# RWKV attention beside a mixture of experts, fp32 on one core: z's transpose into PSUM, GpSimd's differences among its scatters, the last batch routed a round ahead, new orders at the prologue and the seams

## The chip, the cores and the metric

The kernel runs on one core of one Trainium2 chip. The metric is the device time in microseconds (us) of one execution, the median of several. Engines are named as the profile does: PE is TensorE's products and PEld its weight loads, DVE is VectorE, ACT is ScalarE, POOL is GpSimd, SP is SyncE, which here only issues DMAs. The granted clock is the one of TensorE, in parts of 2.4 GHz; its two levels are 1.2 and 2.4 GHz.

## What is computed

The input is x, 8 batches of 512 tokens of 512 channels, fp32. It is normalised to xn, and then out = x + attention(xn) + ffn(xn). Cut to what matters:

```python
# attention: a shifted difference mixed in four proportions, four projections, a scan over time
prev = concatenate([xn[:, 1:2], xn[:, :-1]], axis=1)
xx = prev - xn
k, v, r, g = ((xn + xx * tm_i) @ W_i.T for i in "kvrg")
wkv = scan over t of (a + e^u e^k v) / (b + e^u e^k)          # a, b decay by exp(-exp(time_decay))
o = (sigmoid(r) * wkv * sigmoid(g)) @ Wo.T
attention = layernorm(o) * ln_g + ln_b
# ffn: 32 experts, 4 for each token, at most 256 tokens an expert, and one shared expert
z = w_norm * rmsnorm(xn)
probs = softmax(z @ w_router);  w4, sel = top_k(probs, 4)
position of a token in its expert = how many earlier tokens chose that expert   (dropped from 256 on)
y = (silu(z @ w_gate[e]) * (z @ w_up[e])) @ w_down[e]
ffn = sum of w4 * y over the 4  +  sigmoid(z @ w_shared_gate) * (silu(z @ sw_gate) * (z @ sw_up)) @ sw_down
```

## The kernel before

Each product of fp32 matrices is made of three products of rounded parts. A number is split in a high part, rounded to the type fp32r by ScalarE (`mix_hi`, `z_hi`, `weight_hi`), and a low part, the difference of the number and its high part, which GpSimd or VectorE subtracts (`mix_lo`, `z_lo`, `weight_lo`). TensorE adds low x high, high x low and high x high.

The program has three stages that share SBUF and the eight PSUM banks. The order of the work is written out by hand for each engine, and semaphores tie the engines together; an engine takes its instructions strictly in order.

**Project stage** (0 to 492 us), one round for each batch b. The channels lie in four chunks of 128 (k) and the tokens in four tiles of 128 (j). For the next batch the statistics of x are taken (`norm_stats`), GpSimd makes scales of them (`norm_scales`), ScalarE makes xn (`make_xn`), TensorE transposes it into banks 4 and 5 (`turn_xn`), ScalarE copies it to `xnT` (`keep_turned`), VectorE makes the shifted difference xx (`shift_difference`) and, for K, V, R and G in turn, the mixed operand `mixf` (`make_mix`), which is split into `mix`. `project` runs 24 products for each half of each of K, V, R and G, so 192 a round; a half needs the four chunks of `mix` one after the other, and of K also the gates of the batch before (`make_gate`, which free the banks 0 to 3). z in transposed form is made in four chunks by VectorE (`make_zf`: xnT x norm x the turned row scale), into the two buffers `zf` in SBUF, split into `zT` (hi by ScalarE, lo by VectorE: `make_zT` gives their order), stored for the output stage, and multiplied with the router's weights (`score`) into `sb`, which lies in bank 4. `turn_score`, `choose`, `count` and `assign` turn the scores into slots, and GpSimd issues 16 indirect DMAs a batch, each of which writes 128 token numbers into the table of slots (`scatter`). Of them 7 stand between G's and K's differences (SOME), 4 behind K's, and the last 5 in the next round (MORE = 11).

The rounds are: a first one, three turns of a loop over two rounds each, and a last one. In the last round the work of the last batch is as in the others, but its routing starts with the score behind K's first half, and the first expert's transposes (`first_turn`) stand before the last quarter of G's second half; they need the table, which is read when all scatters have landed, and the rows gathered by it.

**Expert stage** (492 to 928 us), one expert after the other. **Output stage** (928 us to the end), eight rounds of the shared expert in 11 slices f, with the scan, the experts' rows (`gather`, `add_expert`) and the attention's projection between them. In its first round the weights of slice f + 2 are loaded and split (`gate_lo` on VectorE, `weight_lo` on GpSimd, `weight_hi` on ScalarE); in the later ones they are there.

In the profile's rows `mix<-mixf,mix` on POOL is `mix_lo` (L356), `slot_tokens<-token,slot` a scatter, `sr<-sr,bank` on DVE a gate, `zT_lo` the low part of z, `s_wg` on DVE `gate_lo`.

## Time and profile before

| | us |
|---|---|
| time before, median of 3 runs (lowest to highest) | 1764.3 (1762.25 to 1766.29) |
| the profiled execution | 1764.3 |
| its span, first to last instruction | 1762.5 |
| TensorE busy | 1665.3 |
| VectorE busy | 1291.8 |
| GpSimd busy | 899.2 |
| ScalarE busy | 660.3 |
| mean granted clock of TensorE | 0.98 of full |

The profile is one execution. Its rows give start and duration in us from the first instruction on, and in square brackets how long the engine sat idle before and what released it. A group of like instructions stands in one row with its count. The project stage takes 28% of the span, the expert stage 25%, the output stage 47%.

### The profile page before, as it was taken

What the parts mean: (1) busy time and instruction counts of PE and PEld (TensorE: products, weight loads), DVE (VectorE), ACT (ScalarE), POOL (GpSimd) and SP (SyncE); (2) the same over time, 40 slices, a digit from 0 to 9 for tenths busy, and PEclk for the clock granted to TensorE, in tenths of its full rate; (3) what the DMA queues carried; (4) which work ended last, traced back from release to release, by engine and by line L of the source; (5) the groups of instructions that cost most, each with busy time, mean ns of one, the idle gap of its engine ahead of it and who ended that gap; (6) DMA issues with size and microseconds to landing.
All of it is one profiled execution on the core that took longest, in us unless ns stands there. A gap on an engine that the chain in (4) does not pass through costs nothing.

```text
span 1762.5 us, 26296 instructions
## 1 busy us (share of the span) xinstructions
PE 1665.3 (94%) x8496; PEld 1412.4 (80%) x8496; DVE 1291.8 (73%) x1828; ACT 660.3 (37%) x1090; POOL 899.2 (51%) x735
## 2 busy tenths in 40 slices
PE   5888989988899999999998799999999999999998
PEld 4666778777689999999996688888788888888887
DVE  7898898989645555555557978687686768778776
ACT  4444445454356665666653322112121212112121
POOL 6587777778644444444536645244353525344251
PEclk9999999999999999999999999999999999999999
DMA  4353324423466666666677655554554434343431
GB/s 156 144 192 120 120 96 167 167 96 119 148 240 234 219 241 245 242 219 236 245 244 229 209 202 186 173 174 145 187 167 156 129 132 129 123 151 108 155 105 45
DMA packets 123082, 299.38 MB, mean 170 GB/s; under 512 B 20524, under 2 KB 31788, under 8 KB 118384
## 3 DMA queue, kind: packets, MB, share of 16 engines
q1 hardware_dynamic: 103392, 264.34, 42.2%
q0 software_dynamic: 19456, 33.67, 6.7%
q8 instruction: 44, 0.72, 0.2%
q14 instruction: 46, 0.38, 0.1%
q10 hardware_dynamic: 144, 0.26, 0.1%
HBM read 233.61 MB, written 81.36 MB: 179 GB/s over the span
## 4 chain that ended last, share of the span: by engine, by line
PE 71%; DVE 16%; issue 6%; DMA 2%; ACT 2%; POOL 1%; DVEq 0%; SPq 0%; POOLq 0%; ACTq 0%
PE bank L1896 24%; PE bank L1274 15%; PE bank L1910 12%; PE bank L1301 8%; PE bank L1927 5%; PE bank L928 4%; DVE zT_lo L640 3%; DVE mixf L664 2%; PE bank L1266 2%; DMA z_rows<-z 1%; POOL slot_tokens L368 1%; DVE seen L716 1%; DVE xx L656 1%; PE bank L888 1%; DVE zf L633 1%
## 5 line engine op out<-in xcount | busy, mean ns | idle before, releaser
L928 PE MATMUL bank<-mix,w 128*128 128x512 f32 x1536 | 378.0, 405 | 39.4 <-DVE sr L685 32.4
L928 PEld LDWEIGHTS bank<-mix,w 128*128 128x128 f32 x1536 | 298.1, 196 | 110.1 <-DVE sr L685 30.9
L1896 PE MATMUL bank<-s_zT,s_wg 128*128 128x512 f32 x1056 | 256.6, 392 | 12.5 <-DVE s_wg L1800 11.8
L1896 PE MATMUL bank<-s_zT,s_wu 128*128 128x512 f32 x1056 | 255.8, 391 | 3.3 <-DVE s_act_g L1705 1.9
L1910 PE MATMUL bank<-s_wd,s_h 128*128 128x512 f32 x1056 | 254.1, 389 | 0.7 <-DVE s_h L1711 0.6
L1896 PEld LDWEIGHTS bank<-s_zT,s_wg 128*128 128x128 f32 x1056 | 198.7, 189 | 57.2 <-DVE s_wg L1800 14.4
L1896 PEld LDWEIGHTS bank<-s_zT,s_wu 128*128 128x128 f32 x1056 | 198.7, 188 | 46.5 <-POOL s_wu L1568 2.9
L1910 PEld LDWEIGHTS bank<-s_wd,s_h 128*128 128x128 f32 x1056 | 198.3, 188 | 42.7 <-issue 1.0
L1095 POOL TENSOR_TENSOR e_wg<-e_g_in,e_wg 128x1408 fp32r<-128x1408 f32 x31 | 100.3, 3236 | 210.5 <-ACT e_wg L1119 210.5
L356 POOL TENSOR_TENSOR mix<-mixf,mix 128x512 fp32r<-128x512 f32 x124 | 172.1, 1422 | 54.7 <-ACT mix L446 54.6
L1531 POOL DMA_INDIRECT s_picked<-y_rows,s_slot x128 | 142.5, 1114 | 84.3 <-DVE s_total L1761 44.6
L1629 ACT ACTIVATE s_h<-s_act_g 128x512 fp32r<-128x512 f32 x88 | 55.6, 632 | 292.0 <-DVE s_act_g L1705 292.0
L368 POOL DMA_INDIRECT slot_tokens<-token,slot x128 | 138.2, 1079 | 52.0 <-issue 37.6
L1618 ACT ACTIVATE s_act_g<-bank 128x512 f32<-128x512 f32 x88 | 52.6, 597 | 292.0 <-PE bank L1896 292.0
L1274 PE MATMUL bank<-e_xT,e_wg 128*128 128x256 f32 (+1 forms) x1152 | 152.2, 282 | 0.0
L1274 PE MATMUL bank<-e_xT,e_wu 128*128 128x256 f32 (+1 forms) x1152 | 152.1, 282 | 0.0
L1274 PEld LDWEIGHTS bank<-e_xT,e_wg 128*128 128x128 f32 (+1 forms) x1152 | 144.3, 180 | 3.0 <-DVE e_xT L1213 0.4
L1274 PEld LDWEIGHTS bank<-e_xT,e_wu 128*128 128x128 f32 (+1 forms) x1152 | 142.1, 180 | 0.0
L1301 PE MATMUL bank<-e_wd,e_h 128*128 128x512 f32 (+1 forms) x576 | 140.1, 396 | 0.0
L1761 DVE SCALAR_TENSOR_TENSOR s_total<-s_picked,s_rec,s_total 128x512 f32<-128x512 f32 x128 | 132.4, 1034 | 3.4
L1551 POOL TENSOR_TENSOR s_att<-s_gate,s_att 128x512 fp32r<-128x512 f32 x32 | 46.2, 1443 | 165.3 <-ACT s_att L1644 165.3
L446 ACT ACTIVATE mix<-mixf 128x512 fp32r<-128x512 f32 x128 | 77.2, 629 | 133.3 <-DVE mixf L664 127.7
(157 smaller groups left out, 2464.3 us busy)
## 6 DMA issues: line engine op xcount, KB each, us to landing
s_wu<-wu_split SPq DMA_DIRECT2D x77, 512.0 KB, 3.4
e_g_in<-in_w_gate SPq DMA_DIRECT2D x32, 704.0 KB, 4.6
e_u_in<-in_w_up SPq DMA_DIRECT2D x32, 704.0 KB, 6.0
e_d_in<-in_w_down SPq DMA_DIRECT2D x32, 512.0 KB, 6.8
y_rows<-e_y SPq DMA_DIRECT2D x32, 512.0 KB, 2.9
s_zT<-zT_parts SPq DMA_DIRECT2D x16, 1024.0 KB, 7.1
x_in<-in_x SPq DMA_DIRECT2D x32, 256.0 KB, 4.8
zT_parts<-zT_hi SPq DMA_DIRECT2D x8, 1024.0 KB, 6.1
```

Of the source, the lines that this page charges most:

```text
L356: pool.tensor_tensor(mix[:, i % 2, k, 1, :], mixf[:, k, :], mix[:, i % 2, k, 0, :].bitcast(F32), ALU.subtract).then_inc(lo_made, 1)
L368: pool.indirect_dma_start(d["slots"], bass.IndirectOffsetOnAxis(ap=slot[:, at:at + 1], axis=0), token[:, at // TOPK:at // TOPK + 1], None, ...
L446: act.activation(mix[:, i % 2, k, 0, :], mixf[:, k, :], ACT.Copy).then_inc(hi_made, 1)
L928: last = pe.matmul(pj[m][:], w[i][:, w_part, k, m * P:(m + 1) * P], mix[:, i % 2, k, x_part, :], start=(k == 0 and q == 0), stop=(k == KC ...
L1095: pool.tensor_tensor(wg[half][:, 1, :], g_in[half][:], wg[half][:, 0, :].bitcast(F32), ALU.subtract).then_inc(wg_lo, 1)
L1274: last = pe.matmul(gu[f][0:m, which, :], w[half][:, w_part, k * F + f0:k * F + f0 + m], xT[half][:, x_part, k, :], start=(q == 0 and k == ...
L1301: last = pe.matmul(yp[c][:], h[0:m, f, h_part, c * P:(c + 1) * P], wd[half][0:m, w_part, f, :], start=(f == 0 and q == 0), stop=(f == NF - ...
L1531: pool.indirect_dma_start(picked[:, k, :], None, d["y_flat"], bass.IndirectOffsetOnAxis(ap=slot[:, j * TOPK + k:j * TOPK + k + 1], axis=0) ...
L1761: dve.scalar_tensor_tensor(total[:, j, :], picked[:, k, :], rec[:, at:at + 1], total[:, j, :], ALU.mult, ALU.add).then_inc(picked_used, 1)
L1896: last = pe.matmul(into[:], w[:, w_part, k, :], zT[:, x_part, k, :], start=(q == 0 and k == 0), stop=(q == 2 and k == KC - 1))
L1910: last = pe.matmul(yp[j][:], h[:, i, h_part, j * P:(j + 1) * P], wd[f][:, w_part, :], start=(f == 0 and q == 0), stop=(f == NFS - 1 and q ...
L1927: last = pe.matmul(ob[j % 2][:], att[m][:, x_part, j * P:(j + 1) * P], wo[m][:, w_part, :], start=(m == 0 and q == 0), stop=(m == KC - 1 a ...
```

## The change

1. `zf` is no longer in SBUF: it is the pair of PSUM banks 4 and 5, in which the transposes of xn and the score also lie. The transposes of the next batch wait for the subtractions that read it (`zl_made`), and the first of z waits until the score is copied out (`score_kept`).
2. GpSimd's differences of R and K alternate with scatters, one each (`mix_lo_among`); 4 instead of 7 scatters stand before K's differences.
3. Round 1 and round 6 are written out beside the loop (two turns instead of three). In round 1 the four `make_z` of batch 1 stand behind the statistics of batch 2, not before the round; 11 scatters of batch 0 are split by K's differences. In round 6 (`tail`) z of batch 7 is made ahead of K's mixes, its score stands between the halves of G and its turn inside G's second half; in the last round `choose` comes first.
4. In the last round GpSimd makes V's differences only, behind the leftover scatters; R's move to VectorE.
5. The prologue: two of four x tiles are loaded by ScalarE's queue, the constants by SP's, K's first differences by VectorE, the weights of R and G are split in four parts, and V's and z's work changes places.
6. In the first output round the weights' splitting is moved ahead of other work on all three engines, and VectorE's first scan waits for three setup steps instead of four.

```diff
-    zf = at("zf", [P, 2, T], 184)
+    zf = xt
...
         first_round()
-        with eng.Fori(0, B // 2 - 1) as h:
-            one_round(h * 2 + 1, 1)
+        one_round(1, 1, second=True)
+        with eng.Fori(0, B // 2 - 2) as h:
             one_round(h * 2 + 2, 0)
+            one_round(h * 2 + 3, 1)
+        one_round(B - 2, 0, tail=True)
         last_round()
```

SP's queue:

```diff
-        for j in range(NT):
-            load_x(0, j)
-        for i in (K_, V_):
-            load_weight(i)
+        load_x(0, 0)
+        load_x(0, 1)
+        load_weight(K_)
+        sp.dma_start(const[:], d["const"]).then_inc(c_loaded, 16)
+        load_weight(V_)
```

GpSimd:

```diff
+        def mix_lo_among(b, i, of, at):
+
+            for k in range(KC):
+                mix_lo(b, i, (k,))
+                scatter(of, at + k, at + k + 1)
...
-            mix_lo(b, R_)
-            scatter(b - 1, MORE, NT * TOPK)
+            mix_lo_among(b, R_, b - 1, MORE)
+            scatter(b - 1, MORE + KC, NT * TOPK)
             mix_lo(b, G_)
             scatter(b, 0, SOME)
-            mix_lo(b + 1, K_)
-            scatter(b, SOME, MORE)
+            mix_lo_among(b + 1, K_, b, SOME)
+            scatter(b, SOME + KC, MORE)
 
         def last_round():
+            scatter(LAST - 1, MORE, NT * TOPK)
             mix_lo(LAST, V_)
-            scatter(LAST - 1, MORE, NT * TOPK)
-            mix_lo(LAST, R_)
             scatter(LAST, 0, NT * TOPK)
 
-        SOME, MORE = 7, 11
+        SOME, MORE = 4, 11
```

ScalarE, prologue and first round:

```diff
         for k in range(KC):
             mix_hi(0, K_, k)
+            weight_hi(R_, (k,))
...
-            for k in range(KC):
-                mix_hi(0, V_, k)
-            weight_hi(R_)
             exp_k(0, 0)
             exp_k(0, 1)
-            weight_hi(G_)
+            for k in range(KC):
+                mix_hi(0, V_, k)
```

VectorE, z and the prologue:

```diff
+                wait(dve, score_kept, b)
             wait(dve, zl_made, n - 1)
-            dve.scalar_tensor_tensor(zf[:, k % 2, :], xnT[half][:, k, 1:T + 1], norm_col[:, k:k + 1], rb[:],
+            dve.scalar_tensor_tensor(zf[k % 2][:], xnT[half][:, k, 1:T + 1], norm_col[:, k:k + 1], rb[:],
...
         for k in range(KC):
             shift_difference(0, 0, k)
+            if k:
+                mix_lo(0, K_, k - 1)
             make_mix(0, 0, K_, k)
+        mix_lo(0, K_, KC - 1)
+        weight_lo(V_)
```

VectorE, round 1 and round 6:

```diff
             norm_stats(b + 1)
+            if second:
+                for j in range(NT):
+                    make_z(1, 1, j)
...
+            if tail:
+                make_zT(LAST, FIRST_HALF)
             for k in range(KC):
                 make_mix(b + 1, 1 - half, K_, k)
-            make_zT(b + 1, 1 - half)
+            if not tail:
+                make_zT(b + 1, 1 - half)
```

TensorE:

```diff
+            wait(pe, zl_made, b * KC)
...
-            project(b, G_, 1)
+            if tail:
+                score(LAST)
+            project(b, G_, 1, {3: lambda: turn_score(LAST)} if tail else {})
```

The first output round, on GpSimd, ScalarE and VectorE:

```diff
+                if zero(b) and f + 2 < NFS:
+                    weight_lo(U, f + 2)
...
                 hidden_hi(b, half, f)
+                if zero(b) and f + 2 < NFS:
+                    weight_hi(G, f + 2)
+                    weight_hi(U, f + 2)
...
                 hidden_lo(b, half, f)
-                fill(f)
                 if zero(b) and f + 2 < NFS:
                     gate_lo(f + 2)
+                fill(f)
...
-            dve.wait_ge(setup, 4)
+            dve.wait_ge(setup, 3)
```

What stands in a row, at three places. GpSimd between the slots of a batch and the next round, first in the loop of before, where `mix<-mixf,mix` is a difference and `slot_tokens` a scatter:

```order
L368 DMA slot_tokens<-token,slot 8192x1 x7
L355 ISA
L356 TENSOR_TENSOR mix<-mixf,mix 128x512
L355 REGISTER_ALU
L356 TENSOR_TENSOR mix<-mixf,mix 128x512
L355 REGISTER_ALU
L356 TENSOR_TENSOR mix<-mixf,mix 128x512
L355 REGISTER_ALU
L356 TENSOR_TENSOR mix<-mixf,mix 128x512
L368 DMA slot_tokens<-token,slot 8192x1 x4
```

and on GpSimd in the changed kernel, at the same place of round 6:

```order
L372 DMA slot_tokens<-token,slot 8192x1 x4
L358 TENSOR_TENSOR mix<-mixf,mix 128x512
L372 DMA slot_tokens<-token,slot 8192x1
L358 TENSOR_TENSOR mix<-mixf,mix 128x512
L372 DMA slot_tokens<-token,slot 8192x1
L358 TENSOR_TENSOR mix<-mixf,mix 128x512
L372 DMA slot_tokens<-token,slot 8192x1
L358 TENSOR_TENSOR mix<-mixf,mix 128x512
L372 DMA slot_tokens<-token,slot 8192x1 x9
```

Seven scatters ahead of four differences have become four ahead of four pairs; the nine at the end are the pair's last one, three of the same batch and the five that the last round begins with.

VectorE at the end of round 6, before (the loop's end; `zf` and `zT_lo` are z, `sr` the gates):

```order
L664 SCALAR_TENSOR_TENSOR mixf<-xx,keep_const,xnT_66 128x512 x2
L50 REGISTER_ALU
L633 SCALAR_TENSOR_TENSOR zf<-xnT_66,keep_const,bank 128x512 x2
L640 TENSOR_TENSOR zT_lo<-zf,zT_hi 128x512
L633 SCALAR_TENSOR_TENSOR zf<-xnT_66,keep_const,bank 128x512
L640 TENSOR_TENSOR zT_lo<-zf,zT_hi 128x512
L633 SCALAR_TENSOR_TENSOR zf<-xnT_66,keep_const,bank 128x512
L640 TENSOR_TENSOR zT_lo<-zf,zT_hi 128x512 x2
L685 TENSOR_TENSOR sr<-sr,bank 128x512 x4
```

and on VectorE in the changed kernel, from the shifted differences of batch 7 to the first copy of its logits:

```order
L673 TENSOR_TENSOR xx<-xnT_66 128x512 x4
L650 SCALAR_TENSOR_TENSOR bank<-xnT_66,keep_const,bank 128x512 x2
L657 TENSOR_TENSOR zT_lo<-bank,zT_hi 128x512
L650 SCALAR_TENSOR_TENSOR bank<-xnT_66,keep_const,bank 128x512
L657 TENSOR_TENSOR zT_lo<-bank,zT_hi 128x512
L650 SCALAR_TENSOR_TENSOR bank<-xnT_66,keep_const,bank 128x512
L657 TENSOR_TENSOR zT_lo<-bank,zT_hi 128x512 x2
L681 SCALAR_TENSOR_TENSOR mixf<-xx,keep_const,xnT_66 128x512 x4
L702 TENSOR_TENSOR sr<-sr,bank 128x512 x2
L709 COPY lg<-bank 128x136
```

z reads and writes a bank now and has moved ahead of K's mixes, and `choose` (from `lg` on) has moved between the first and the second pair of gates.

TensorE in the last round of before (`w_56` to `w_59` are the weights of K, V, R and G, `zT_lo` and `zT_hi` the score, `oh` its turn, `chosen` and `seen` the count):

```order
L928 MATMUL bank<-mix,w_56 128x512 x24
L888 MATMUL bank<-zT_lo,wr 68x512 x4
L888 MATMUL bank<-zT_hi,wr 68x512 x4
L928 MATMUL bank<-mix,w_56 128x512 x12
L897 MATMUL bank<-keep_const,oh 128x68 x4
L928 MATMUL bank<-mix,w_56 128x512 x12
L928 MATMUL bank<-mix,w_57 128x512 x18
L905 MATMUL bank<-chosen,before 128x128
L906 MATMUL bank<-seen,ones 128x128
L928 MATMUL bank<-mix,w_57 128x512 x30
```

and on TensorE in the changed kernel, from the middle of G of batch 6 to V of batch 7:

```order
L957 MATMUL bank<-mix,w_59 128x512 x24
L917 MATMUL bank<-zT_lo,wr 68x512 x4
L917 MATMUL bank<-zT_hi,wr 68x512 x4
L957 MATMUL bank<-mix,w_59 128x512 x18
L926 MATMUL bank<-keep_const,oh 128x68 x4
L957 MATMUL bank<-mix,w_59 128x512 x6
L957 MATMUL bank<-mix,w_56 128x512 x30
L934 MATMUL bank<-chosen,before 128x128
L935 MATMUL bank<-seen,ones 128x128
L957 MATMUL bank<-mix,w_56 128x512 x18
L957 MATMUL bank<-mix,w_57 128x512 x48
```

The score of batch 7 has moved from K of batch 7 into G of batch 6, and the count from V into K.

## Rows read from the trace of the kernel before

**Rows 1.** The page, busy time, share of the span and instructions of each engine.

```profile
PE 1665.3 (94%) x8496; PEld 1412.4 (80%) x8496; DVE 1291.8 (73%) x1828; ACT 660.3 (37%) x1090; POOL 899.2 (51%) x735
```

**Rows 2.** Windows by stage: length, busy by engine, PEclk, DMA share, GB/s.

```profile
0.00:152.30 152.30, 111.79 (x472) 86.28 (x472) 131.23 (x219) 68.37 (x110) 102.83 (x96) 0.94 0.39 142
152.30:429.30 277.00, 253.28 (x1131) 205.78 (x1131) 247.14 (x461) 131.11 (x227) 215.55 (x201) 0.95 0.34 129
429.30:492.60 63.30, 52.36 (x215) 41.91 (x215) 38.85 (x77) 22.34 (x34) 39.99 (x35) 0.88 0.47 169
492.60:927.50 434.90, 434.90 (x3129) 410.86 (x3129) 239.53 (x383) 268.31 (x446) 196.79 (x96) 1.00 0.68 239
927.50:1050.00 122.50, 107.37 (x446) 84.64 (x445) 100.04 (x93) 38.12 (x66) 67.07 (x57) 0.97 0.64 211
```

**Rows 3.** Timeline of PE, a steady round: start, us, what [idle before <-releaser].

```profile
207.38 7.36 PE L928 MATMUL bank<-mix,w 128*128 128x512 f32 x24 [4.06 <-DVE sr L685]
...
235.61 22.04 PE L928 MATMUL bank<-mix,w 128*128 128x512 f32 x96
```

**Rows 4.** Timeline of DVE, the same stretch.

```profile
227.01 3.86 DVE L716 TENSOR_TENSOR seen<-seen,chosen 128x32 bf16<-128x32 bf16 x4
...
244.26 0.17 DVE L738 TENSOR_TENSOR slot<-s,s 128x16 uint32<-128x16 f32 x1
...
254.18 5.82 DVE L640 TENSOR_TENSOR zT_lo<-zf,zT_hi 128x512 fp32r<-128x512 f32 x1
```

**Rows 5.** Timeline of POOL, the same stretch.

```profile
204.17 1.26 POOL L368 DMA_INDIRECT slot_tokens<-token,slot  x1 [0.17 <-issue]
...
213.22 5.87 POOL L356 TENSOR_TENSOR mix<-mixf,mix 128x512 fp32r<-128x512 f32 x4 [3.87 <-ACT mix L446]
...
254.43 5.00 POOL L356 TENSOR_TENSOR mix<-mixf,mix 128x512 fp32r<-128x512 f32 x4
```

**Rows 6.** Groups by line: count, busy us, mean ns of one, idle before.

```profile
L368 POOL DMA_INDIRECT slot_tokens<-token,slot x128 | 138.2, 1079 | 52.0 <-issue 37.6 <-DVE slot L738 14.3
...
L1213 DVE TENSOR_TENSOR e_xT<-bank,e_xT 128x512 fp32r<-128x512 f32 x64 | 41.2, 686 | 29.6 <-ACT e_xT L1134 29.6
...
L680 DVE TENSOR_TENSOR ekv<-ek,bank 128x512 f32<-128x512 f32 x32 | 20.4, 678 | 0.0
```

**Rows 7.** Timeline of PE, the end of the last round.

```profile
488.61 1.98 PE L1266 MATMUL bank<-keep_const,e_rows 128*128 128x128 f32 x8 [8.23 <-DMA e_rows<-z_rows,keep_index]
```

**Rows 8.** Timeline of POOL, the end of the last round.

```profile
478.75 0.97 POOL L368 DMA_INDIRECT slot_tokens<-token,slot  x1 [0.30 <-issue]
```

**Rows 9.** Timeline of all engines, the opening.

```profile
14.64 0.43 SPq L271 DMA_DIRECT2D wr_staged<-in_Wr  x1
...
21.32 4.36 PE L928 MATMUL bank<-mix,w 128*128 128x512 f32 x12 [3.95 <-POOL mix L356]
```

**Rows 10.** Timeline of DVE, the first round.

```profile
37.38 3.81 DVE L640 TENSOR_TENSOR zT_lo<-zf,zT_hi 128x512 fp32r<-128x512 f32 x1 [1.17 <-ACT zT_hi L439]
...
58.86 3.44 DVE L613 SCALAR_TENSOR_TENSOR z<-xn,r,norm_w 128x512 f32<-128x512 f32 x2 [2.51 <-DMA z_rows<-z]
```

**Rows 11.** Timeline of PE, the first two rounds.

```profile
48.32 1.98 PE L888 MATMUL bank<-zT_lo,wr 128*68 128x512 f32 x4 [7.61 <-DVE zT_lo L640]
...
98.29 7.42 PE L928 MATMUL bank<-mix,w 128*128 128x512 f32 x24 [2.26 <-DVE sr L685]
```

**Rows 12.** DMA issues of the first 60 us: line, count, KB, us to landing.

```profile
wr_staged<-in_Wr SPq DMA_DIRECT2D x1, 1024.0 KB, 7.1
```

**Rows 13.** Timeline of DVE, the first output round.

```profile
934.78 1.23 DVE L1728 TENSOR_TENSOR_SCAN s_b_sum<-keep_decay,s_ek 128x512 f32<-128x512 f32 x1 [5.16 <-POOL s_picked L1580]
...
998.23 4.69 DVE L1711 TENSOR_TENSOR s_h<-s_act_g,s_h 128x512 fp32r<-128x512 f32 x1 [0.70 <-ACT s_h L1629]
```

**Rows 14.** Timeline of PE, the same stretch.

```profile
937.85 4.46 PE L1896 MATMUL bank<-s_zT,s_wu 128*128 128x512 f32 x12 [1.92 <-DVE s_act_g L1705]
...
1009.89 0.50 PE L1896 MATMUL bank<-s_zT,s_wg 128*128 128x512 f32 x1 [3.90 <-DVE s_wg L1800]
```

More of the change, by code:

```diff
@@ L294, in first_round, with one_round @@
                 load_x(2, j)
-            for j in range(NT):
-                store_z(1, j)
-        def one_round(b, half):
+        def one_round(b, half, second=False, tail=False):
+            if second:
+                store_zT(1)
             store_gate(b - 1)
-            store_zT(b)
+            if not second:
+                store_zT(b)
+            if second:
+                for j in range(NT):
+                    store_z(1, j)
             store_ek(b)
-            if not (isinstance(b, int) and b + 2 >= B):
+            if not tail:
                 for j in range(NT):
@@ L526, in first_round, with one_round @@
                 z_hi(1, k)
-        def one_round(b, half):
+        def one_round(b, half, second=False, tail=False):
             gate_g(b - 1, 2)
@@ L554, in one_round @@
             gate_r(b, 1)
+            if tail:
+                for k in range(KC):
+                    z_hi(LAST, k)
             mix_hi(b + 1, K_, 0)
@@ L560, in one_round @@
             mix_hi(b + 1, K_, 3)
-            for k in range(KC):
-                z_hi(b + 1, k)
+            if tail:
+                keep_score(LAST)
+            else:
+                for k in range(KC):
+                    z_hi(b + 1, k)
             gate_g(b, 0)
@@ L776, in first_round @@
             keep_scales(0, 0)
+            for k in range(KC):
+                make_mix(0, 0, R_, k)
+            make_ekv(0, 0)
+            make_ekv(0, 1)
             dve.wait_ge(n_loaded, 16)
@@ L779, in first_round @@
             make_z(0, 0, 1)
-            make_ekv(0, 0)
-            make_ekv(0, 1)
-            for k in range(KC):
-                make_mix(0, 0, R_, k)
+            make_ekv(0, 2)
+            make_ekv(0, 3)
             make_z(0, 0, 2)
             make_z(0, 0, 3)
-            make_ekv(0, 2)
-            make_ekv(0, 3)
             choose(0)
@@ L801, in first_round, with one_round @@
             keep_scales(1, 1)
-            for j in range(NT):
-                make_z(1, 1, j)
-        def one_round(b, half):
+        def one_round(b, half, second=False, tail=False):
             make_gate(b - 1, 2)
@@ L810, in one_round @@
             norm_stats(b + 1)
+            if second:
+                for j in range(NT):
+                    make_z(1, 1, j)
             for k in range(KC):
@@ L829, in one_round @@
                 shift_difference(b + 1, 1 - half, k)
+            if tail:
+                make_zT(LAST, FIRST_HALF)
             for k in range(KC):
                 make_mix(b + 1, 1 - half, K_, k)
-            make_zT(b + 1, 1 - half)
+            if not tail:
+                make_zT(b + 1, 1 - half)
             make_gate(b, 0)
@@ L836, in last_round @@
         def last_round():
+            choose(LAST)
             make_gate(LAST - 1, 2)
@@ L840, in last_round @@
                 make_mix(LAST, FIRST_HALF, V_, k)
-            for k in range(KC):
-                make_mix(LAST, FIRST_HALF, R_, k)
-            choose(LAST)
             assign(LAST)
-            make_ekv(LAST, 0)
-            make_ekv(LAST, 1)
+            for pair in ((0, 1), (2, 3)):
+                for k in pair:
+                    make_mix(LAST, FIRST_HALF, R_, k)
+                if pair[0] == 0:
+                    make_ekv(LAST, 0)
+                    make_ekv(LAST, 1)
+                for k in pair:
+                    mix_lo(LAST, R_, k)
+            make_ekv(LAST, 2)
+            make_ekv(LAST, 3)
             for k in range(KC):
                 make_mix(LAST, FIRST_HALF, G_, k)
-            make_ekv(LAST, 2)
-            make_ekv(LAST, 3)
             for k in range(KC):
@@ L954, in first_round, with one_round @@
             project(0, G_, 1)
-        def one_round(b, half):
+        def one_round(b, half, second=False, tail=False):
             project(b, K_, 0)
@@ L1675, in one_round @@
                 if zero(b) and f + 2 < NFS:
-                    for which in (G, U, D):
-                        weight_hi(which, f + 2)
+                    weight_hi(D, f + 2)
                 if zero(b) and f == 1:
```

94 lines of the change are left out of this document (45 added, 49 removed).

## Prediction

> **What bounds the kernel now.** I read the page first: TensorE is busy 94% of the span, VectorE 73%, GpSimd 51% [rows 1]. That is an average over stages, so the windows by stage come next [rows 2]. The eight rounds of the first stage have the losses: in the five steady rounds (K of batch 2 to K of batch 7, 277.0 us, 55.4 each) TensorE is idle 23.7 us and its mean granted clock is 0.95; in the opening 40.5 us are idle at 0.94, in the last round 10.9 at 0.88, and in the first output round 15.1 at 0.97. From 492.6 to 927.5 TensorE is never idle, so the expert stage can't give anything, and the output rounds after 1050.0 are not touched.
>
> In a steady round the PE timeline shows where the loss sits: the K product starts 4.06 us late, released by the gate product on VectorE (`sr`, L685), and its 24 products take 7.36 us, while 96 later ones take 22.04, that is 5.51 per 24 [rows 3]. So the engine comes out of the idle time at the lower level of its clock (1.2 instead of 2.4 GHz for some of it) and loses another 1.85 us. From 207.38 to the end of G at 257.65 are 50.27 us; less 1.85 the engine needs **48.4 us** a round.
>
> Why the gate is late stands in the VectorE timeline: one `zT_lo` subtraction, at 254.18, takes 5.82 us [rows 4], while GpSimd runs four differences, of 5.00 us together, beside it [rows 5]. VectorE work with an operand in PSUM is not stretched beside GpSimd: `ekv<-ek,bank` has a mean of 678 ns over 32, `e_xT<-bank,e_xT` 686 over 64 [rows 6].
>
> **The change, part by part.** *z in PSUM.* The same 32 multiplications and 32 subtractions run. The subtraction has the form of `e_xT`, so I price it at 0.69; once a round 5.82 - 0.69 = 5.13 us go. By the Trainium skill, page "SBUF — State Buffer", section "SBUF: two separate sides", GpSimd and a VectorE instruction with two SBUF inputs exclude each other for a whole instruction, so a PSUM operand frees it; that agrees with the rows. But by the same rule it would wait for one GpSimd instruction, a quarter of 5.0 us, not for four; then only 1.25 us a round would be saved. The row with 5.82 us decides, and the sum takes 5.13. The new waits (xn's transposes for `zl_made`, z for `score_kept`) ask for events half a round old; I cost them at nothing. If that cover were gone, the transposes would wait out the subtractions, about 3 us.
>
> *The steady round.* VectorE sets it now: 55.4 - 5.13 = 50.3 us. What is late next? TensorE needs 48.4. GpSimd is busy 215.55 / 5 = 43.1 [rows 2], and 16 scatters add 0.3 each between them: 47.9, without its waits for others. So VectorE's 50.3 stays the longest, by a thin margin. The new GpSimd order doesn't add work: from `slot` on, 4 scatters of about 1.3, then four pairs of difference and scatter at 1.25 + 1.43. The last K difference comes 5.3 + 3 x 2.68 + 1.25 = 14.6 us after `slot` (244.4); before it was 254.43 + 5.00 = 259.4, 15.0 after it. TensorE wants it 4.1 us into K, at T + 52.5 in terms of the K start T; it is ready at T + 37.1 + 14.6 = T + 51.7. That fits with 0.8 us to spare. GpSimd's V differences begin about 1 us later than now (213.22 has 3.87 idle before it). Spread differences stretch the `seen` additions (3.86 for four [rows 4], nearly one difference each) less often: perhaps 1 us better. I take **50.3** (48.8 to 53). For four rounds: 221.5 to 201.2, -20.3.
>
> *Round 6, which scores batch 7.* It gets 8 score products and 4 transposes (2.2 us, an estimate: 8 x 0.23 by the 96 in 22.04, and 0.4) and they stand ahead of the last quarter of G; z of batch 7 is then made ahead of the K mixes, after some 43 us of VectorE work, when TensorE arrives at about the same time. 48.4 + 2.2 + 1.9 for meeting late = 52.5 against 55.5, -3.0.
>
> *Last round.* Now 63.3 us, of which 8.23 idle for the gathered rows [rows 7], 2.7 idle elsewhere, the rest slow clock and work. The chain behind the 8.23 is 16 scatters in a row, the last at 478.75 [rows 8], then table, index, gather: first transpose at 488.61, 9.86 after the last scatter starts. After: `slot` is ready some 16 us into the round, but GpSimd first runs four leftover scatters, five more of batch 6 and then the V differences. It leaves the tail's four at T + 8, the five at T + 14.5, V from 14.5 to 19.5. TensorE wants V at T + 12.8, so it **loses about 3 to 5 us in a place where it loses nothing now**. The 16 scatters of batch 7 start at T + 19.7, the last one at 38.9, the transposes at T + 48.8; TensorE comes there at T + 47.2. Adding 4.0 from the first transpose to the first expert product gives 52.8: -10.5 (-4 to -14). `choose` ahead of the gates also holds K's second half by some 2 us; that is in it.
>
> *Opening.* To K of batch 2: 152.3 us. The first product starts at 21.3 [rows 9]. From there two rounds at 48.4 would end at 118, so 34 us can be had at most. Of those, VectorE's two `zT_lo` beside GpSimd's weight differences (3.81 for the first of them [rows 10]) leave TensorE idle for 7.61, and z's stores and slow clock cost 2.26 idle and 7.42 - 5.51 = 1.9 in K's second half [rows 11]. Following the new order by these durations: K runs from 20 to 34, V's first half to 39.5 (V's low weights, on VectorE, are ready at 29), score to 41.5, V's second half to 47, R with its transposes to 60, G to 72.6. Then K of batch 1 is paced by pairs of difference and scatter and ends its first half at 80, and score(1) starts there instead of at 92.4. In round 1 VectorE sets the pace: z's four products now stand behind the statistics, and K of batch 2 comes at 125 by VectorE, 130 with what such a chain leaves out. -22 (-12 to -28). A cost in it: ScalarE's rounding of R's first quarter stands behind the first K rounding and needs the weights, which are issued at 14.64 and land 7.1 later, at 21.7 [rows 9, 12]. That delays K's second chunk by 1.5 us; counted.
>
> *Seam to the output.* VectorE waits 5.16 us for GpSimd's memset of `picked`, the fourth setup step, where it will ask for three [rows 13], and TensorE then waits 1.92 and takes 4.46 us for 12 products, 2.8 at full clock [rows 14]: -3.5. Of the remaining idle time much is released by `gate_lo` (3.90 at 1009.89), but VectorE's chain is full there, with stretched instructions as the 4.69 at 998.23 [rows 13]. Moving `gate_lo` ahead of the fill work lets TensorE do a gate product earlier and then wait for `hidden`; I give it 2.5. The roundings moved ahead of `silu` can hold ScalarE while pieces arrive, so -6 in all (+3 to -14).
>
> **Sum.** -20.3 - 3.0 - 10.5 - 22 - 6 = -61.8. The profiled execution is 1764.3 us (span 1762.5, 1.8 around it), which is the median of the three runs. 1764.3 - 61.8 = 1702.5, say **1703 us**.
>
> **Rivals.**
> 1. *GpSimd becomes the bound.* For: 47.9 us plus waits for ScalarE's roundings is close to 50, and pairs leave it no room. A period of 53 gives 4 x 53 + 55 = 267 instead of 277 (-10), -5 in the last round, -22 and -6: **1721**. Against: it waits 3.87 us before V now.
> 2. *The stall moves.* K's and V's mixes read two SBUF operands. If one of them waits out the differences that z's subtraction waited for, rounds stay at 55; only the opening, the last round and the seam gain: 1764.3 - 2 - 14 - 8 - 6 = **1734**. Against: the differences are single between scatters, so one waits 1.25 at most.
> 3. *The opening gives little,* held by z's stores (VectorE waits 2.51 for one [rows 10]) or R's weights: -10 instead of -22, **1715**.
> 4. *Slower.* Alternation sets VectorE's and GpSimd's instructions against each other all the time. Four V differences take 5.87 instead of 5.0 where mixes run beside them [rows 5]. If all four groups do (+0.9 each) and 16 scatters grow by 0.4 each, GpSimd's round is 47.9 + 3.6 + 6.4 = 57.9: +2.5 a round over now, five times, and the other terms shrink to -8 together: **1769**. It decides from 0.3 us more a scatter. Against: a scatter's mean is 1.08 us over all 128 now [rows 6].
>
> **How the numbers follow.** Forecast 0.66, rival 1 0.16, rival 2 0.05, rival 3 0.09, rival 4 0.04. The range should leave out 2 in 10: the forecast's own terms go from 1678 to 1739 if all ends come together, 1687 to 1722 without that; with rivals 1 and 3 inside and rival 2 at its edge I give 1687 to 1733. A measurement of this kernel tells about 0.2% (3.5 us) from no change. Faster by more: forecast and rivals 1 to 3, 0.95 less a little for several going wrong, 0.94; slower 0.04; within 0.02.
>
> **What would show it.** `zT_lo` at a mean near 0.7 us instead of 1.9, no long one; K starts 50 us apart with next to no idle before them and the clock near 1.0 in the rounds; K of batch 2 near 130, the first expert product near 436; TensorE waiting for V's differences in the last round; the setup wait gone. Wrong if K starts stay 53 or more apart, if GpSimd is released by no one in the rounds and TensorE waits for its `mix`, or if the first output round still takes 122 us.

## The result, and the profile after

The changed kernel takes **1735.1 us** (median, 1733.8 to 1736.0), the kernel before 1764.1 in the same measurement; the ratio is 0.983, with an interval of 0.982 to 0.985. It is faster by 29 us, not by the 61.8 that the forecast gave, and lies 2 us above the upper end of its range. The profiled execution has a span of 1734.2 us.

Page of after, part 1, against [rows 1]:

```profile
PE 1653.1 (95%) x8496; PEld 1402.8 (81%) x8496; DVE 1275.4 (74%) x1836; ACT 661.5 (38%) x1093; POOL 885.7 (51%) x733
```

Windows of after, cut at the places of [rows 2]: the opening up to K of batch 2 in two windows, four steady rounds, round 6, the last round, the experts, the first output round. Columns as there:

```profile
17.20:80.14 62.94, 51.91 (x226) 40.10 (x226) 55.79 (x104) 32.34 (x54) 38.41 (x33) 0.97 0.38 137
80.14:141.92 61.78, 51.52 (x227) 41.10 (x227) 58.38 (x107) 30.28 (x53) 50.25 (x46) 0.94 0.36 136
141.92:352.37 210.45, 198.67 (x904) 159.24 (x905) 193.71 (x369) 104.86 (x182) 172.17 (x161) 0.99 0.39 140
352.37:407.90 55.53, 52.36 (x238) 41.93 (x239) 50.53 (x99) 26.61 (x47) 42.17 (x40) 0.97 0.39 152
407.90:468.04 60.14, 48.72 (x204) 38.99 (x202) 36.16 (x75) 22.76 (x34) 37.38 (x35) 0.91 0.41 143
468.04:903.00 434.96, 434.96 (x3128) 410.90 (x3129) 239.56 (x383) 268.36 (x446) 196.80 (x96) 1.00 0.67 239
903.00:1020.80 117.80, 105.07 (x446) 83.60 (x446) 101.32 (x93) 37.53 (x66) 67.20 (x57) 0.99 0.68 219
```

So every stage gained less than forecast, the seam by the least: opening 10.4 us (152.3 to 141.9; forecast 22), four steady rounds 10.7 (221.1 to 210.45; forecast 20.3), round 6 and the last round 3.5 together (119.1 to 115.7; forecast 13.5), the first output round 4.7 (122.5 to 117.8; forecast 6 with what lies around it). The experts take 434.96 as before.

The one step on which most rested is right. Group of `zT_lo` over the whole run, by line: count, busy us, mean ns; it was 1894 ns before the change:

```profile
L657 DVE TENSOR_TENSOR zT_lo<-bank,zT_hi 128x512 fp32r<-128x512 f32 x32 | 22.0, 688 | 0.6
```

But a round gained less than these 5.13 us. Timeline of a steady round of after, PE, then DVE, then POOL, to be held against [rows 3 to 5]:

```profile
193.62 7.34 PE L957 MATMUL bank<-mix,w 128*128 128x512 f32 x24 [2.34 <-DVE sr L702]
...
221.82 22.58 PE L957 MATMUL bank<-mix,w 128*128 128x512 f32 x96
246.72 3.50 PE L957 MATMUL bank<-mix,w 128*128 128x512 f32 x14 [2.32 <-DVE sr L702]
```

```profile
201.50 6.23 DVE L681 SCALAR_TENSOR_TENSOR mixf<-xx,keep_const,xnT 128x512 f32<-128x512 f32 x4 [0.62 <-POOL mix L358]
...
213.12 2.70 DVE L733 TENSOR_TENSOR seen<-seen,chosen 128x32 bf16<-128x32 bf16 x4
215.93 2.69 DVE L629 SCALAR_TENSOR_TENSOR z<-xn,r,norm_w 128x512 f32<-128x512 f32 x2
...
220.92 0.79 DVE L629 SCALAR_TENSOR_TENSOR z<-xn,r,norm_w 128x512 f32<-128x512 f32 x1 [1.11 <-DMA z_rows<-z]
...
232.18 0.17 DVE L755 TENSOR_TENSOR slot<-s,s 128x16 uint32<-128x16 f32 x1
...
236.38 4.13 DVE L681 SCALAR_TENSOR_TENSOR mixf<-xx,keep_const,xnT 128x512 f32<-128x512 f32 x4
```

```profile
238.65 1.30 POOL L358 TENSOR_TENSOR mix<-mixf,mix 128x512 fp32r<-128x512 f32 x1
240.12 1.26 POOL L372 DMA_INDIRECT slot_tokens<-token,slot  x1 [0.17 <-issue]
```

From `slot` to the next K start it is 14.5 us, where it was 18.55 (244.26 to 262.81 before): 4.0 less instead of 5.13, since the four K mixes take 4.13 us and not 2.74. From `seen` to `slot` it is 19.1 instead of 17.25. The additions of `seen` got 1.16 shorter, as forecast, but the two z behind them 1.27 longer (1.42 before), and VectorE then waits 1.11 for z's store and stands another 1.60 in front of the fourth z, released by nothing that the profile shows; this 1.60 stands in one of the four rounds. The other rounds are 51.7, 53.7 and 51.95 us long.

The first row of VectorE above is R's four mixes, which read two SBUF operands. GpSimd's block of V's differences (200.15 to 205.19) runs beside them, and they take 6.23 to 6.24 us in three of the four rounds. Before, in the same place:

```profile
218.20 3.43 DVE L664 SCALAR_TENSOR_TENSOR mixf<-xx,keep_const,xnT 128x512 f32<-128x512 f32 x4
```

They end 14.1 us after K's start as they did before (207.73 - 193.62; 221.63 - 207.38 is 14.25): VectorE comes to them earlier and loses it there.

The end of the last round, PE, DVE and POOL:

```profile
422.73 33.16 PE L957 MATMUL bank<-mix,w 128*128 128x512 f32 x138 [3.26 <-POOL mix L358]
464.05 1.98 PE L1297 MATMUL bank<-keep_const,e_rows 128*128 128x128 f32 x8 [8.16 <-DMA e_rows<-z_rows,keep_index]
```

```profile
422.61 3.78 DVE L754 CAST token<-keep_const 128x4 uint32<-128x4 f32 x1 [3.93 <-DMA slot_tokens<-token,slot]
```

```profile
421.38 4.97 POOL L358 TENSOR_TENSOR mix<-mixf,mix 128x512 fp32r<-128x512 f32 x4
427.30 0.99 POOL L372 DMA_INDIRECT slot_tokens<-token,slot  x1 [0.94 <-DVE slot L755]
434.23 0.98 POOL L372 DMA_INDIRECT slot_tokens<-token,slot  x1 [5.94 <-issue]
...
454.22 0.97 POOL L372 DMA_INDIRECT slot_tokens<-token,slot  x1 [0.30 <-issue]
```

The first scatter stands where the forecast put it (19.4 us after K's start at 407.9; 19.7 forecast), the last one does not: 26.9 us behind the first, not 19.2. So the transposes still wait 8.16 us, as in [rows 7].

### The profile page after: what moved, and what is told of

Same layout as the page of the kernel before. It is cut to its first block, busy times and chain, and to the rows that moved or that the text cites. A ratio compares the mean times of both kernels' runs of the same rounds, so it can differ in the third digit from the quotient of the medians.

```text
span 1734.2 us, 26081 instructions
## 1 busy us (share of the span) xinstructions
PE 1653.1 (95%) x8496; PEld 1402.8 (81%) x8496; DVE 1275.4 (74%) x1836; ACT 661.5 (38%) x1093; POOL 885.7 (51%) x733
## 4 chain that ended last, share of the span: by engine, by line
PE 69%; DVE 14%; issue 8%; POOL 4%; DMA 3%; ACT 2%; DVEq 0%; SPq 0%; POOLq 0%; ACTq 0%
PE bank L1930 24%; PE bank L1305 16%; PE bank L1944 12%; PE bank L1332 8%; PE bank L1961 5%; DVE mixf L681 3%; POOL slot_tokens L372 2%; PE bank L1297 2%; PE bank L957 2%; DMA z_rows<-z 1%; POOL mix L358 1%; DVE bank L650 1%; DVE z L629 1%; DVE s_wg L1834 1%; DVE ekv L697 1%
## 5 line engine op out<-in xcount | busy, mean ns | idle before, releaser
L957 PE MATMUL bank<-mix,w 128*128 128x512 f32 x1536 | 369.4, 398 | 27.5 <-DVE sr L702 11.0
L957 PEld LDWEIGHTS bank<-mix,w 128*128 128x128 f32 x1536 | 289.3, 191 | 97.9 <-DVE sr L702 10.6
L1930 PE MATMUL bank<-s_zT,s_wu 128*128 128x512 f32 x1056 | 256.3, 392 | 13.5 <-DVE s_act_g L1739 11.5
L358 POOL TENSOR_TENSOR mix<-mixf,mix 128x512 fp32r<-128x512 f32 x116 | 154.8, 1353 | 51.5 <-ACT mix L455 50.5
```

The lines of the kernel that those rows point to most:

```text
L358: pool.tensor_tensor(mix[:, i % 2, k, 1, :], mixf[:, k, :], mix[:, i % 2, k, 0, :].bitcast(F32), ALU.subtract).then_inc(lo_made, 1)
L957: last = pe.matmul(pj[m][:], w[i][:, w_part, k, m * P:(m + 1) * P], mix[:, i % 2, k, x_part, :], start=(k == 0 and q == 0), stop=(k == KC ...
L1930: last = pe.matmul(into[:], w[:, w_part, k, :], zT[:, x_part, k, :], start=(q == 0 and k == 0), stop=(q == 2 and k == KC - 1))
```

## The experiments

Each kernel was timed beside the kernel before on the same chip; ratios and intervals are to that one.

### z in PSUM alone, and everything but it

The first run takes the kernel before and moves only z:

```diff
-    zf = at("zf", [P, 2, T], 184)
...
+    zf = xt
...
+                wait(dve, score_kept, b)
...
+            wait(pe, zl_made, b * KC)
```

> The kernel before with one edit of the change alone: zf lies in the two PSUM banks, with its two waits; GpSimd keeps its blocks of four differences. Theory 1 (the pairs of difference and scatter took back what z in PSUM gave): zT_lo falls from 5.82 to 0.7 us in each round, K's four mixes stay at 2.74 us, the K starts stand 50.3 apart, and the first round gains its two long subtractions (6.6 us). Sum 1764 - 6.6 - 6 x 5 = about 1728, faster than the changed kernel (1735). Theory 2 (the stretch moves to other VectorE work wherever GpSimd's differences stand): rounds of 53, about 1745, slower than the changed kernel.

Measured: **1735.1 us**, ratio 0.983 (0.982 to 0.985). That is the time of the whole change. Neither number was met: the rounds behave nearly as theory 1 says (51.2 us, not 50.3), but the last round is 66.4 us long, 3.1 more than before. Timeline of PE and of DVE in this run:

```profile
140.17 5.73 PE L930 MATMUL bank<-mix,w 128*128 128x512 f32 x24 [1.32 <-DVE sr L686]
191.45 5.73 PE L930 MATMUL bank<-mix,w 128*128 128x512 f32 x24 [1.34 <-DVE sr L686]
...
235.24 6.06 PE L930 MATMUL bank<-mix,w 128*128 128x512 f32 x24 [0.60 <-ACT sr L461]
242.63 5.76 PE L930 MATMUL bank<-mix,w 128*128 128x512 f32 x24 [1.33 <-DVE sr L686]
```

```profile
233.29 2.74 DVE L665 SCALAR_TENSOR_TENSOR mixf<-xx,keep_const,xnT 128x512 f32<-128x512 f32 x4
```

K's half starts at the full clock now (5.73 for 24, not 7.36). K of batch 2 comes at 140.17, earlier than in the changed kernel (141.92), and K of batch 6 at 344.93 (352.37). The other parts of the change thus cost 7.4 us up to there. The last two rounds (115.7 us there, 117.8 here) and the seam gave it back. In the last round VectorE now meets R's block of differences with an instruction on 4 numbers a partition, in the middle of the choice, and TensorE waits 7.13 us for the count:

```profile
414.99 4.89 DVE L714 TENSOR_SCALAR keep_const<-keep_const 128x4 f32<-128x4 f32 x1
```

The second run leaves everything of the change but z: `zf` is in SBUF again, the two waits are gone.

> The changed kernel with zf back in SBUF and without the two new waits; all its orders stay. Theory 1 (a VectorE instruction waits out the whole run of GpSimd instructions that follow each other without a gap; between pairs there is one): zT_lo waits for one difference, 1.3 us more, in one or two of four, so a round is 1.3 to 2.6 longer and the time 1743 to 1750. Theory 2 (scatters hold VectorE out as well as differences do): zT_lo waits 5 us as before, 55 a round, about 1760.

Measured: **1755.2 us**, 0.996 (0.995 to 0.997). So z in PSUM is worth 20 us inside the change. The time lies between the theories, above the 1750 of theory 1; the mechanism is that of theory 1, since no instruction waits 5 us:

```profile
247.29 1.39 DVE L656 TENSOR_TENSOR zT_lo<-zf,zT_hi 128x512 fp32r<-128x512 f32 x1
...
249.38 2.05 DVE L656 TENSOR_TENSOR zT_lo<-zf,zT_hi 128x512 fp32r<-128x512 f32 x1
...
252.13 2.63 DVE L656 TENSOR_TENSOR zT_lo<-zf,zT_hi 128x512 fp32r<-128x512 f32 x2
```

Here the four take 6.07 us, against 2.82 with z in PSUM and 7.98 in the kernel before (0.69, 5.82 and 1.47 for two); I had counted one or two that wait, and it is three. Pairs spread the wait over several instructions; with z in SBUF that helps a little, with z in PSUM there is nothing left to help.

### Pairs or blocks on GpSimd

K's differences in one block again, behind seven scatters:

```diff
-            scatter(b, 0, SOME)
-            mix_lo_among(b + 1, K_, b, SOME)
-            scatter(b, SOME + KC, MORE)
+            scatter(b, 0, SOME + 3)
+            mix_lo(b + 1, K_)
+            scatter(b, SOME + 3, MORE)
```

> The changed kernel with K's differences in one block behind seven scatters, as before; R's pairs stay. Theory 1 (K's pairs cost VectorE 1.4 us a round, 4.15 instead of 2.74 for four mixes; a block would fall beside z and the gates, which have an operand in PSUM): rounds of 50.3 instead of 51.7, six times, about 1727. Theory 2 (the block stretches other work as much as the pairs do): 1735, no change.

Measured: **1729.5 us**, 0.981 (0.979 to 0.982): theory 1, with 5.6 of its 8 us. (The gain is against 1735.1; the intervals of the two kernels touch, and the rounds show it.) The rounds are 51.5 us (K of batch 2 at 140.65, of batch 6 at 346.48). DVE in one of them: the K mixes are back at 2.73, and a wait for the store of z shows up.

```profile
220.94 1.48 DVE L629 SCALAR_TENSOR_TENSOR z<-xn,r,norm_w 128x512 f32<-128x512 f32 x2 [2.41 <-DMA z_rows<-z]
...
234.72 2.73 DVE L681 SCALAR_TENSOR_TENSOR mixf<-xx,keep_const,xnT 128x512 f32<-128x512 f32 x4
```

R's differences in a block as well (`mix_lo(b, R_)`, then the five scatters):

> The kernel of the run with K's block (1729.5 us) with R's differences in a block too, as before the change. Theory 1 (R's pairs cost nothing net: the stretch falls on the two z of the first pair, 2.69 instead of 1.41, instead of on the additions of seen, 3.87 instead of 2.70): 1729.5, rounds of 51.2. Theory 2 (the pairs also make the z wait longer for their stores, 2.41 against 0.50 in a round): one of the four rounds gets 1 us shorter, 1727 to 1729. Rival (R's block makes TensorE wait): over 1731.

Measured: **1725.4 us**, 0.977 (0.975 to 0.979), 4 less. DVE:

```profile
210.19 3.87 DVE L733 TENSOR_TENSOR seen<-seen,chosen 128x32 bf16<-128x32 bf16 x4
214.16 1.41 DVE L629 SCALAR_TENSOR_TENSOR z<-xn,r,norm_w 128x512 f32<-128x512 f32 x2
...
218.30 1.51 DVE L629 SCALAR_TENSOR_TENSOR z<-xn,r,norm_w 128x512 f32<-128x512 f32 x2 [1.52 <-DMA z_rows<-z]
```

`seen` and the first two z take 5.28 us together, 5.39 in pairs; the wait for the store is 0.9 shorter. K of batch 6 comes at 343.62 instead of 346.48; of these 2.9 us, 1.8 lie ahead of K of batch 2 (about 138.9 instead of 140.65), and the rounds are 51.2 us. Theory 2, with a larger effect than said; the two intervals just touch.

### The opening

The first round's K differences in a block too, on the kernel with K's block:

```diff
-            mix_lo_among(1, K_, 0, SOME)
-            scatter(0, SOME + KC, MORE)
+            mix_lo(1, K_)
+            scatter(0, SOME, MORE)
```

> The kernel of the run with K's block (1729.5 us) with the first round's K differences in a block as well, behind four scatters. In the changed kernel TensorE takes K's first half of round 1 at the pace of pairs, 2.74 us a chunk instead of 1.66. Theory 1 (the pairs set the opening too): score of batch 1 2.5 us earlier, near 86.8, K of batch 2 near 138, 1727. Theory 2 (VectorE is the bound of the opening: busy 114 of the 125 us from 17.2 on, so what TensorE gains is lost again at the count of batch 1): K of batch 2 at 140.6 or later, 1729.5.

Measured: **1728.4 us**, 0.980 (0.978 to 0.982), against 1729.5. PE:

```profile
86.61 1.14 PE L917 MATMUL bank<-zT_lo,wr 128*68 128x512 f32 x4 [1.18 <-DVE zT_lo L657]
...
114.45 0.29 PE L934 MATMUL bank<-chosen,before 128*128 128x128 bf16 x1 [6.00 <-DVE seen L733]
```

The score of batch 1 comes 2.7 us earlier than in the changed kernel (89.32), its count only 0.5 (114.95, where TensorE waits 5.96). Part of that isn't the edit's: the count of batch 0, which stands ahead of it, is 1.6 us earlier already (62.85, there 64.42). Counted from it, the score comes 1.1 us earlier and the count of batch 1 1.1 us later (51.6, there 50.5), and the score of batch 2 stands at 146.12, in the kernel with K's block at 146.26. VectorE's chain to the choice of batch 1 swallows what TensorE gains: theory 2. The 1.1 us of time are within the noise.

What in that chain is long was asked next, on the joined kernel below. Of z of batch 1 by rows only 8 of 512 channels are made, so this kernel leaves the others out:

> The joined kernel in which the four multiplications that make z of batch 1 by rows take 8 of the 512 channels (so the expert inputs of batch 1 are not computed); all waits stay. Asks what bounds the opening. Theory 1 (VectorE's chain in round 1, z, R's mixes, then the choice, which TensorE waits 6 us for at the count of batch 1): these four took 4.94 + 1.43 us; the count and K of batch 2 come 3 to 5 us earlier. Theory 2 (TensorE or GpSimd): K of batch 2 stays where it is.

Measured: **1723.4 us**, 0.977 (0.976 to 0.978); the joined kernel has 1721.6. The count comes 1.1 us earlier and no more, the score of batch 2 1.2 (143.66, there 144.90): less than theory 1 said, more than theory 2. DVE and POOL in this run:

```profile
94.54 4.56 DVE L629 SCALAR_TENSOR_TENSOR z<-xn,r,norm_w 128x8 f32<-128x8 f32 x2
101.15 0.23 DVE L629 SCALAR_TENSOR_TENSOR z<-xn,r,norm_w 128x8 f32<-128x8 f32 x1 [2.05 <-DMA z_rows<-z]
```

```profile
93.90 5.03 POOL L358 TENSOR_TENSOR mix<-mixf,mix 128x512 fp32r<-128x512 f32 x4
```

Two multiplications of 8 channels take 4.56 us, two of 512 took 5.61 there (a single one of 8 takes 0.23): the first waits until GpSimd's run of four is over, at 98.9. Cutting the work of a waiting instruction gives little, and the wait for the store grows from 1.51 to 2.05 us.

The other wait in that chain is the store. z by rows gets four buffers instead of two, the new ones where `zf` lay:

```diff
-    z = at("z", [P, 2, C], 176)
+    z = at("z", [P, NT, C], 176)
...
-            wait(dve, z_stored[j % 2], (b * 2 + j // 2) * 16)
+            wait(dve, z_stored[j], b * 16)
```

> The joined kernel with four SBUF buffers for z by rows instead of two (the second two in the place that zf left), so that VectorE never waits for a store of z. Theory 1 (VectorE sets the rounds and the opening, so each wait for a store counts): the waits are 0.5 to 2.4 us in a round and 3.8 in the opening; 3 to 8 us less than the joined kernel. Theory 2 (TensorE sets the rounds at 51.2 now: ACT's gate of R and the slow gate product leave it about 2 us idle): under 2 us.

Measured: **1718.6 us**, 0.974 (0.973 to 0.976), 3 less than the joined kernel; the two intervals overlap a little, so the rows have to show it. PE:

```profile
111.14 0.23 PE L934 MATMUL bank<-chosen,before 128*128 128x128 bf16 x1 [0.21 <-DVE seen L733]
...
137.40 5.73 PE L957 MATMUL bank<-mix,w 128*128 128x512 f32 x24 [1.33 <-DVE sr L702]
...
188.18 5.74 PE L957 MATMUL bank<-mix,w 128*128 128x512 f32 x24 [1.33 <-DVE sr L702]
...
201.05 0.41 PE L926 MATMUL bank<-keep_const,oh 68*128 68x68 f32 x4
```

DVE, R's mixes in the round that starts at 188.18:

```profile
196.68 6.24 DVE L681 SCALAR_TENSOR_TENSOR mixf<-xx,keep_const,xnT 128x512 f32<-128x512 f32 x4 [1.24 <-POOL mix L358]
```

The count comes 2.4 us earlier than in the joined kernel (3.4, counted from the count of batch 0) and waits for nearly nothing. Theory 1 at its lower end: rounds of 50.8 us, there 51.2.

### The last round

V's differences of the last round on VectorE, on the changed kernel:

```diff
             scatter(LAST - 1, MORE, NT * TOPK)
-            mix_lo(LAST, V_)
             scatter(LAST, 0, NT * TOPK)
...
+            for k in range(KC):
+                mix_lo(LAST, V_, k)          # VectorE, behind V's mixes
             assign(LAST)
```

> The changed kernel with V's differences of the last round on VectorE instead of GpSimd. Theory 1 (GpSimd's four V differences cost twice: TensorE waits 3.26 us for them, and the copy of token numbers, 3.78 us beside them, holds the slots and with them all 16 scatters): slot near 423 instead of 426.3, the scatters start 3 to 4 us earlier, TensorE's 3.26 gone, first transposes of the expert stage near 460 instead of 464, about 1731. The idle 5.94 us behind the first scatter stays if it comes from the loads of the expert's weights that run then; if it belongs to the V differences it goes too, then 1726. Theory 2 (the last round is bound elsewhere): 1735.

Measured: **1735.8 us**, 0.983 (0.981 to 0.985): no gain. DVE:

```profile
426.54 0.17 DVE L753 CAST token<-keep_const 128x4 uint32<-128x4 f32 x1 [6.71 <-DMA slot_tokens<-token,slot]
```

The copy of the token numbers takes 0.17 us now instead of 3.78, so GpSimd's V differences had stretched it. But it starts no sooner: it waits until the scatters of batch 6 have landed, 7.1 us after the last of them starts (419.48); in the changed kernel it was 2.2 (420.41 to 422.61). Beside them run the store of e^k and the 3 MB of the first expert's weights, issued from 418.3 on; that these make the landing late is a guess at this point. So SP's order was changed, on the kernel with K's block:

```diff
+            first_weights()
             store_gate(LAST - 1)
             store_ek(LAST)
-            first_weights()
```

> The kernel of the run with K's block (1729.5 us) with one more edit: in the last round SP issues the first expert's weights (3 MB) ahead of the stores of the gates and of e^k, some 15 us earlier. Theory 1 (the 6.44 us in which GpSimd stands between the first and the second scatter of batch 7, and the late landing of scatters, come from these loads, which fill the 16 DMA engines from 417 to 434): with the loads over before the scatters begin, the gap falls to 0.3 to 2.9 us, the first transposes of the expert stage come 3.5 to 6 us earlier, 1723.5 to 1726. Theory 2 (the gap belongs to something else, it stands in every kernel so far with at least 2.94): gap 6.4, 1729.5.

Measured: **1726.8 us**, 0.977 (0.976 to 0.979), 2.7 less. POOL, first of the kernel with K's block alone, then with the loads early:

```profile
420.78 0.99 POOL L372 DMA_INDIRECT slot_tokens<-token,slot  x1 [0.94 <-DVE slot L755]
428.21 0.98 POOL L372 DMA_INDIRECT slot_tokens<-token,slot  x1 [6.44 <-issue]
```

```profile
422.06 0.99 POOL L372 DMA_INDIRECT slot_tokens<-token,slot  x1 [0.94 <-DVE slot L755]
426.00 1.32 POOL L372 DMA_INDIRECT slot_tokens<-token,slot  x1 [2.95 <-issue]
...
447.23 0.97 POOL L372 DMA_INDIRECT slot_tokens<-token,slot  x1 [0.30 <-issue]
```

The idle time behind the first scatter falls by 3.5 us and TensorE's wait for the gathered rows from 10.71 to 8.13. The rest, 2.95, stands there however early the loads are; what it is I didn't find. With the loads early V's differences were moved once more, on the joined kernel:

> The joined kernel with V's differences of the last round on VectorE. Alone on the changed kernel this gave nothing: the copy of the token numbers then waited 6.71 us for the scatters of batch 6 to land, beside 4 MB of other transfers. Theory 1 (that wait came from the weights' loads): with the loads early the slot is ready near 16 us into the last round instead of 17.4 and the transposes come 1.5 us earlier, -1.5. Theory 2 (VectorE's own four differences, 3 us, put slot as late): 0 to +1.

Measured: **1722.7 us**, 0.977 (0.976 to 0.979), against 1721.6. From K of batch 6 to the transposes it is 106.5 us instead of 107.2, half of the expected gain, and the time doesn't show it: theory 2. The stretch behind the transposes is 4.5 us longer in this profile, which the edit doesn't touch. Over the profiles of the eleven kernels with the new seam this stretch goes from 1268.3 (joined) to 1276.5 us (V's on VectorE, on the changed kernel), with the same code; why stays open, and a difference of that size between two profiles says nothing of an edit.

### The seam alone

The output round's edits of the change on the kernel before, nothing else:

> The kernel before with one part of the change alone: the new orders of the first output round on GpSimd, ScalarE and VectorE, and three setup steps instead of four. In the changed kernel the stretch from the first expert product to the gate product of the second output round was 4.7 us shorter. Theory 1 (that is this edit): 1764.3 - 4.7 = 1759.6. Theory 2 (the stretch is shorter for other reasons): 1764.

Measured: **1760.0 us**, 0.997 (0.995 to 0.998): 5.2 less, theory 1. TensorE's largest wait in the first output round (total, times, longest), before, then in this run:

```profile
PE bank L1896 <- DVE s_wg L1800: 11.8, 5, 3.9
```

```profile
PE bank L1899 <- DVE s_act_g L1708: 10.9, 6, 2.4
```

The wait changed its name and nearly kept its size; of the one for `s_wg` 0.2 us are left. Most was gained early in the round: TensorE's tenth group of 12 products starts 26.8 us after the first (925.72 to 952.49), where it was 30.9 (927.58 to 958.45), 4.1 of the 4.9 us that the round got shorter. There VectorE's first scan of the stage, released 5.16 us late by `picked` in [rows 13], follows its neighbour without idle time. The run holds the shorter setup wait and the new orders together, so how much is owed to which isn't shown.

### The edits joined

K's and R's blocks, the first round's block and the early loads, in one kernel:

> The changed kernel with four edits together: K's and R's differences in blocks, the first round's K differences in a block behind four scatters, and the first expert's weights issued early. Sum of what the single runs gave: 1735.1 - 5.6 (K's block) - 4.0 (R's block) - 1.1 (first round) - 2.7 (weights) = 1721.7. Rival (K's and R's blocks had already taken what the other two can give): 1725.

Measured: **1721.6 us**, 0.976 (0.975 to 0.978). The single gains add up. That they do so to 0.1 us is luck: each of them is known to 2 to 4 us, and one, the first round's 1.1, may be nothing. With the four buffers of z, 1718.6 us is the fastest kernel of the study, 1% faster than the changed one.

## Why the forecast was too large

- **z in PSUM, steady rounds** (5.13 us a round): right. In the run with z alone the stretch from the first scatter to the next K start falls from 17.55 (245.26 to 262.81) to 12.37 us (230.26 to 242.63), by 5.18. An instruction that waits, waits for GpSimd's run of four to its end. The Trainium skill, page "SBUF — State Buffer", section "SBUF: two separate sides", has an exclusive lock held for one whole instruction; the rows agree with it as to which instructions are freed, not as to how long the others wait.
- **The round's 50.3 us**: too low by 0.9 even with blocks (51.2). TensorE waits 0.6 us for ScalarE's gate and 1.3 for the gate product in each round, and VectorE for z's stores; with four buffers it is 50.8. What is left was overlooked by the forecast and by the runs: R's mixes beside V's block, 6.23 to 6.25 us in three of four rounds with blocks and four buffers too. There they end 14.7 us into the round (202.92 after 188.18), and TensorE has the scores turned at 13.3 (201.46), so the choice starts 1.4 us late. That is an estimate of what another place for V's block could give a round; no run moved it.
- **"The new GpSimd order doesn't add work … perhaps 1 us better"**: this step failed. `seen` gained its 1.16, but I priced no other VectorE instruction that now meets a single difference. The K mixes (+1.4) and the z (+1.3) did. The worry was in rival 2, and I had dismissed it with "one waits 1.25 at most": that is the price in each round, and I left it out of the sum. Rounds of 51.7 to 53.7 are between the forecast and rival 2's 55. GpSimd was not the bound; TensorE waited for its `mix` in no steady round. Blocks in both places give 9.7 us back, 5.7 of them in the four rounds and 3.0 in the opening.
- **Opening** (22): mis-sized. Two long `zT_lo` in the first round and one in the second make 11.7, and z alone measured 12.2. The 10 us for the new order were TensorE's arrivals added up, while the windows show VectorE busy 114.2 of 124.7 us there, time in which its instructions wait for GpSimd included; it was the bound. A gain of TensorE's was lost there (the first round's block), a wait taken from VectorE was not (the four buffers). Rival 3 gave -10 for it, the size that came out, but named VectorE's wait for z's stores and R's weights. Of these the stores were part of it.
- **Last round** (-10.5): the term was mis-sized. V's wait (3.26 us) and the first scatter came as forecast. From the first of the 16 scatters to the last I took 15 x 1.28 = 19.2 us, though the timeline of before had them at 23.5 (455.24 to the row of [rows 8]), 2.94 of it the idle time behind the first; they took 26.9. The first expert's loads fell on them: with the loads early the 16 take 25.2 us, 27.7 without (K's block in both). So 7.7 us were missing in the chain behind which TensorE waits, and the early start of the routing went into it.
- **Round 6** (-3.0): nothing came, 55.5 us. TensorE waits 3.17 us for z of batch 7 ahead of its score.
- **Seam** (-6): about right, 4.7 to 5.2.
- **Slower by alternation** (rival 4) saw that alternation costs, but put the cost on GpSimd: a scatter's mean rose from 1.08 to 1.10 us, not by 0.4, and GpSimd was not the bound. The cost fell on VectorE.
- **The time itself** lies 1 us from rival 2's 1734, by luck. Rival 2 had 2 us for the rounds, 14 for the opening, 8 for round 6 and the last and 6 for the seam; measured are 10.7, 10.4, 3.5 and 4.7. Its mechanism is there in part: K's mixes wait, for one difference a round and not for four.

## What to carry to other kernels

When an instruction waits out another engine's run, free that instruction and then ask where the run should stand so that only freed instructions lie beside it. Here a solid block beside z's PSUM work was better than pairs that meet everything, and the block that stayed beside R's mixes was overlooked. Before crediting a new order with TensorE's idle time, look whether another engine is full in the same window. And take a serial chain from its first to its last row, not from a mean times a count; the idle time inside it is part of it.

## What was not expected of the hardware

- A VectorE instruction can wait much longer than it works: two multiplications of 8 channels took 4.56 us beside a run of four differences, and a copy of 4 numbers a partition with a single SBUF input 3.78 us (until 426.39; GpSimd's run ended at 426.35). Two operands in SBUF are not needed for it.
- GpSimd stood still behind the first of the last 16 scatters in all fourteen kernels: 2.94 to 3.10 us in nine, in which the weights' loads were first issued 8.7 us or more before that scatter; 3.41 in the one with z back in SBUF (7.9 us before it); 5.94 to 6.86 in the four (the changed one, those with K's block, with both blocks and with the first round's block) in which they were issued 3 to 5 us before it. The loads explain 3 to 4 us of it; the 2.95 is open.
- A scatter whose landing was waited for took 7.1 us with these loads issued 0.6 us ahead of it, and 2.2 where they were issued 2.0 us behind it. That the loads are the cause is likely, not shown: the store of e^k is issued just ahead of them and moves with them.
